# A graph layer on one core: GpSimd's gathers wait in one place instead of three, and TensorE runs two more products per group

## What is computed

```python
h = relu(layernorm(x))                                  # 12500 x 128
l1 = linear(h)                                          # per node: lin_table
w  = silu(silu(rbf(dist) @ fc_w1) @ fc_w2) @ fc_w3      # per edge, 4 x 32 weights
g  = l1[edge_src]                                       # gather, 200000 rows of 128
msg = products of w, g and edge_sh                      # per edge, 256 values
agg = segment_sum(msg, edge_dst) / count                # edge_dst is sorted
out = x + linear(h) + tanh(agg_s @ alpha_w) * linear2(agg)
```

## Time and profile before

| | |
|---|---|
| runs, us | 2487.68, 2496.71, 2497.35; median 2496.71 |
| profiled execution, span | 2483.8 us |
| mean granted TensorE clock | 0.826 of full speed |
| TensorE matmuls busy | 1811.4 us, 73%, 7969 records |
| VectorE busy | 1783.0 us, 72% |
| ScalarE busy | 1199.1 us, 48% |
| GpSimd busy | 1578.4 us, 64% |
| DMA engines, mean | 63 GB/s moved |

### The profile page before, as it was taken

How to read it: one execution, slowest core, us unless ns; L and a number is a source line. 1 busy time by engine, 2 the same in 40 slices (tenths; PEclk the granted TensorE clock), 3 DMA queues, 4 the chain that set the end, 5 groups by cost and what they waited for, 6 DMA issues and landing times. The chain is left out here.

```text
span 2483.8 us, 34021 instructions
## 1 busy us (share of the span) xinstructions
PE 1811.4 (73%) x7969; PEld 1174.2 (47%) x7969; DVE 1783.0 (72%) x4669; ACT 1199.1 (48%) x3310; POOL 1578.4 (64%) x1624
## 2 busy tenths in 40 slices
PE   6577777787777777767677767667787776877777
PEld 6344444454444444444444434444554444544544
DVE  8577767767776777767676667767677776777777
ACT  6354545455454555444444344445444444445443
POOL 7566666666666666666666666666666666666563
PEclk9588878878888887788787878888888888888889
DMA  7322222222222222222122222222222222222222
GB/s 214 70 64 67 56 64 66 66 56 66 66 59 62 67 65 56 55 48 50 46 50 48 48 48 49 54 50 64 57 67 62 59 65 66 53 64 61 59 66 55
DMA packets 347699, 155.73 MB, mean 63 GB/s; under 512 B 237983, under 2 KB 322048, under 8 KB 347584
## 3 DMA queue, kind: packets, MB, share of 16 engines
q0 software_dynamic: 50016, 102.51, 15.7%
q1 hardware_dynamic: 296938, 51.75, 11.4%
q10 hardware_dynamic: 630, 0.29, 0.0%
HBM read 134.27 MB, written 20.15 MB: 62 GB/s over the span
## 5 line engine op out<-in xcount | busy, mean ns | idle before, releaser
L970 POOL DMA_INDIRECT lin_g<-lin_table,src_ix x1563 | 1530.0, 979 | 865.1 <-issue 441.5
L1157 ACT ACTIVATE lin_sh<-lin_g,harm 128x128 f32<-128x128 f32 x1563 | 483.8, 396 | 94.6 <-DMA lin_g<-lin_table,src_ix 87.6
L1040 PE MATMUL ps_sums<-near_sums,far_hot 128*128 128x257 f32 x520 | 208.0, 488 | 440.8 <-DVE agg L1474 206.0
L1030 PE MATMUL ps_near<-msg,onehot 128*64 128x257 f32 x3126 | 507.5, 471 | 1.2 <-DVE msg L1423 1.2
L1018 PE MATMUL ps_w<-w,h 128*128 128x256 f32 x1566 | 462.6, 440 | 28.2 <-ACT key_all L1167 18.5
L1018 PEld LDWEIGHTS ps_w<-w,h 128*128 128x128 f32 x1566 | 395.3, 272 | 135.4 <-issue 44.9
L999 PE MATMUL ps_h<-rbf,w 32*128 32x192 f32 x1044 | 277.0, 390 | 138.0 <-issue 67.1
L1415 DVE TENSOR_TENSOR msg<-lin_sh,key_all 128x576 f32<-128x576 f32 (+1 forms) x261 | 197.3, 756 | 249.9 <-ACT key_all L1167 209.5
L1167 ACT ACTIVATE key_all<-ps_w 128x768 f32<-128x768 f32 x261 | 213.5, 818 | 305.2 <-remote 188.6
L1030 PEld LDWEIGHTS ps_near<-msg,onehot 128*64 128x64 f32 x3126 | 241.3, 164 | 230.6 <-issue 175.7
L1383 DVE TENSOR_TENSOR lin_sh<-lin_g,ps_meta 128x576 f32<-128x576 f32 (+1 forms) x261 | 196.6, 753 | 212.2 <-DMA lin_g<-lin_table,src_ix 207.0
(11 more groups left out here) (175 smaller groups left out, 1655.2 us busy)
## 6 DMA issues: line engine op xcount, KB each, us to landing
lin_g<-lin_table,src_ix POOLq DMA_INDIRECT x1563
dist_in<-in_edge_weight SPq DMA_DIRECT2D x67, 96.0 KB
lin_table<-lin_out SPq DMA_DIRECT2D x24, 256.0 KB, 2.6
x_in<-in_x SPq DMA_DIRECT2D x24, 256.0 KB
skip_table<-x_in SPq DMA_DIRECT2D x24, 256.0 KB
xq<-in_x SPq DMA_DIRECT2D x23, 256.0 KB, 3.9
harm<-in_edge_attr SPq DMA_DIRECT2D x66, 48.0 KB
x_in<-skip_table SPq DMA_DIRECT2D x8, 256.0 KB
```

The costliest lines, as they stand in the source:

```text
L970: pool.indirect_dma_start(slot_tiles(s, u)[rows, t, :], None, lin_table, bass.IndirectOffsetOnAxis(ap=src_ix[rows, s.phase, u, col:col + 1 ...
L1030: mm = pe.matmul(ps_near[half * NEAR:(half + 1) * NEAR, 0:MSG + 1], onehot[:, u, t, :], msg[:, u % 2, t, :], start=(j == 0), stop=(j == PA ...
L1040: pe.matmul(ps_nodes(i), far_hot[:, u, :], near_sums[:, u % 2, :], start=True, stop=True).then_inc(sums_ready, 1)
L1157: last = act.activation(lin_sh0[:, u % 2, j, :], slot_tiles(s, u)[:, j, :], ACT.Copy, scale=harm[:, s.phase, u, harm_col(j):harm_col(j) + 1])
```

## The change

GpSimd's `gather` loses the waits before the third and the fifth DMA of a group, each with the `nop` that carried it; the wait at the head stays. TensorE's `layer3` gets two further products of `w2` (128 x 128) with `w3` (128 x 256), written to the last two of `ps_w`'s eight column blocks, which nothing reads. They stand after the wait for `w_copied` and ahead of layer3's own three products. They take part in every call of layer3, 261 in all.

```diff
+WARM = 2
@@ gather, on GpSimd
                             for k, t in enumerate(tiles):
-                                if not first and k == 2:
-                                    pool.wait_ge(h2_done, s.i * SLOTS + u)
-                                    pool.nop(nofuse=True)
-                                if not first and k == 4:
-                                    pool.wait_ge(sums_ready, s.i * SLOTS + u - SLOTS + 1)
-                                    pool.nop(nofuse=True)
                                 col = t % HALVES * PAIRS + t // HALVES
@@ layer3, on TensorE
                             at_least(pe, w_copied, i * SLOTS + u)
+                            for _ in range(WARM):
+                                pe.matmul(ps_w[:, TILES * P:], w2[:], w3[:], start=True, stop=True)
                             cols = h2[:, u % 2, :].rearrange("p (c j) -> p j c", j=PAIRS)
```

## The result

The changed kernel takes 2676.64 us, median of four runs (2668.99 to 2694.38), against 2496.42 us for the kernel before in the same job: a ratio of 1.0736, 95% interval 1.0695 to 1.0778. It is 7.4% slower. The forecast was 2460 us with 2580 as the upper end of the range; the time is outside, on the side of the "own pauses" rival, which had been given 2541 us for one group in eight and 2621 for one in four.

The account below looks back on a forecast made before the run. No engine is full; waits hold the loop, with 396 us of GpSimd pauses. Waits -21 and -16 us, products 0: 2483.8 - 37 = 2447 span, forecast 2460 us since the profiled execution is 12.9 below the median; range 2400 to 2580.

Parts of the forecast that it names:

- own pauses: Rival, chance 0.28: products delay the near product, GpSimd pauses after six gathers, not twelve, 2.6 us each; 2541 or 2621 us.
- Late completions: Reading of two cycles: TensorE's completions reach others up to 9.5 us late during unbroken gathers; a 2 us pause releases them.
- So a pause moves to a head rather than vanishing. What is gained is regularity.: GpSimd's removed waits: pauses only at group heads, 8.93 us a group against 9.06, or 9.31 in the last turns.
- the sum's -37 us: Gain from removing GpSimd's two waits: -21 us over turns 2 to 41, -16 us over the last 22.
- That pause also lets the completions out.: GpSimd's third and fifth gathers: a binding wait costs up to a pause, which also releases TensorE's completions; no separate size.
- 0 on the path: Two products ahead of layer 3: 253 to 483 us of TensorE work, hidden by late-seen completions, so costing 0.
- The clock: TensorE: extra products shorten idle gaps, mean clock rises above 0.82 to 0.85; where it holds, layer 3 is 1.3 us shorter.
- The two fast rivals: Removed waits were pure cost, 2429 us, chance 0.06; TensorE's clock stays at 1.00 nearly throughout, 2407 us, chance 0.06.
- Nothing changes: Rival, chance 0.20: GpSimd's pauses only move and the products are hidden, 2497 us.

## Why the prediction was wrong

*Late completions.* The reading that TensorE's completions are seen late while gathers follow one another held. It was inferred from two cycles, and the run with half the gathers showed it: no late copy of ps_near where there had been 80. By what mechanism it happens no run shows.

*"So a pause moves to a head rather than vanishing. What is gained is regularity."* This step failed, for 2.6% by itself. I took 8.93 us a group from two cycles of twelve gathers, one behind the other, and gave it to every group. In the kernel before, 43 of the 185 runs between pauses of over 1 us are of twelve gathers. Twelve gathers per pause need the near product after each flush to be out before the next run of gathers shuts completions in, or at least to be over when GpSimd stops. Without the waits 76 of the 164 runs between pauses of over 1 us were of six gathers. By the rival's price, 171 pauses instead of 130 (one for two groups) are 41 x 2.6 = 107 us over the forecast, 2567; measured 2556. So the sum's -37 us should have been a loss of 63. The rival's mechanism, pauses six gathers apart, was the right one, and I gave it 0.28 for the wrong reason: it came without the products, too.

*"That pause also lets the completions out."* I had named this effect of a stop in mid-group and then valued it at nothing: I priced a stop at its length only. It lets layer 3's copy, the messages and the next near product run beside the gathers still to come. Without it they run in the pause itself: the near product had not begun in 30 pauses, 5.1 us long in the mean, where there had been 3, and one stop put back brought them to 3, 8 or 11.

*The products "0 on the path".* With both waits kept they cost 33 of their 329 us where I took 0, a small error of size. But the 0 was taken from the cycle of the kernel before, whose cover the other half of the change removes. In the changed kernel they cost 119 us. That is not their own time inside pauses: of the 57 pauses with the near product not begun they reach into 20, for 19 us in all. They come ahead of layer 3, so its copy, the messages and the near product come later, and the near product had not begun in 57 pauses instead of 30 (297 us instead of 154). The two edits should have been costed in order, the second against a trace in which the first was done.

*The clock.* The products raised the granted clock alone (0.826 to 0.863) and with the waits gone (0.804 to 0.844). The latter is hardly above the clock of before. In the cycle read it was 0.50 where the pause was made, with the products as well (854 to 862 us above, after TensorE had idled for 7.03 us). The gain in TensorE's own work was real, 161 us with all waits and 163 in the changed kernel against the kernel before, but no kernel with the products was shorter than the same kernel without them. By the Trainium skill's page "TensorE: Matmul & The Clock Gate" (section on what is actually happening) activity releases the throttle, and the trace agrees; that this pays for the products, as I had drawn from it, no run shows.

*The size.* 203 pauses instead of 130 are 73 x 2.6 = 190 us, 2650; that a pause is 596 / 203 = 2.94 us long instead of 2.6 adds 69; the gathers' own records give back 29. That makes 2690, measured 2676.64. This is a sum made afterwards from the changed kernel's own counts, so it checks the price of a pause and explains nothing of their number. In the range I had stopped the rival at one extra pause in five or six groups, where it was one in 3.6.

*The two fast rivals* are out: the idle time attributed to the two removed waits came back more than once over, and the clock stayed at 0.84. *Nothing changes* is out as well.

What stays open: why the completions are held while GpSimd issues gathers, and from how many in a row on. The time since gathers resumed doesn't settle it: of the near products that ended 3.75 to 5 us after a resumption, with ScalarE free, none of 6 was seen late without the waits, and 21 of 22 in the changed kernel. Open are also whether a higher clock alone would shorten the long pauses, and why the products' cost with only the third wait kept (76 us) lies midway, where I had expected it near the 33 us of both waits.

## What to carry to other kernels

A wait that seems to hold an engine for nothing may be what lets another engine's results through, so count what runs beside it before taking it out, and test that edit alone. Before pricing work as hidden, take its cover from a trace in which the other edits are already made: the same two products cost 33 us or 119. And where one or two good cycles carry a forecast, count in the trace of before how many cycles have that form.

## What the runs showed that I had not expected

Completions of TensorE reached ScalarE some 9 us late at worst in the cycles read, while GpSimd issued gathers one after another. In the changed kernel 32 near products ended while GpSimd stood still with ScalarE free, and none was copied more than 1 us late; of 28 that ended within a run of gathers 24 were. Halving the rows of each gather (from 49 to 28 GB/s) changed little of it (80 late copies of ps_near with either), halving the number of gathers took it away. The completions of ScalarE and VectorE reached TensorE without such a delay. A gather of 64 rows costs GpSimd 0.900 us where one of 128 costs 0.944. A memset between two gathers took 0.12 us out of their 0.30 us distance, and the pace within a run stayed at 1.25 us.
